# Making the second product of each gate/up pair by seven half-size products

## The reference

```python
def bitlinear(x, w):
    scale = mean(abs(w))
    return x @ (round(clip(w / (scale + EPS), -1, 1)) * scale).T
out = x + bitlinear(bitlinear(y, w_gate) * bitlinear(y, w_up), w_down)
```

## Time and profile before

| | us |
|---|---|
| median of 3 runs (1727.34 to 1729.59) | 1727.45 |
| span of the profiled execution | 1726.1 |
| PE busy | 1707.7 |
| DVE busy | 1096.0 |
| ACT busy | 575.6 |
| POOL busy | 28.0 |

### The profile page before, as it was taken

The page is one execution under the profiler, slowest core; times in us unless marked ns, Lnnn a source line. Parts: engine busy times, 40 slices in busy tenths (PEclk is TensorE's granted clock), DMA queues, the critical chain, the costliest instruction groups (busy, mean ns, idle before and its releaser), DMA issues.

```text
span 1726.1 us, 31355 instructions
## 1 busy us (share of the span) xinstructions
PE 1707.7 (99%) x12424; PEld 1215.6 (70%) x12424; DVE 1096.0 (63%) x1786; ACT 575.6 (33%) x921; POOL 28.0 (2%) x59
## 2 busy tenths in 40 slices
PE   6999999999999999999999999999999999999999
PEld 5554545968769596795958768596776959678684
DVE  6898895555766468554685646755576545855464
ACT  6887732312333133230333213231233313323120
POOL 0010000000000000000000000000000000000000
PEclk9999999999999999999999999999999999999999
DMA  8666626312242032420224211331223313132021
GB/s 342 249 229 239 221 96 219 121 44 97 76 148 96 22 108 77 168 66 22 107 102 164 65 75 54 129 137 43 97 76 126 101 40 108 65 124 79 29 87 49
DMA packets 59735, 194.06 MB, mean 112 GB/s; under 512 B 5280, under 2 KB 5600, under 8 KB 59584
## 3 DMA queue, kind: packets, MB, share of 16 engines
q1 hardware_dynamic: 56432, 177.49, 28.9%
q0 software_dynamic: 2560, 14.36, 2.2%
q10 hardware_dynamic: 592, 0.09, 0.0%
HBM read 160.90 MB, written 31.01 MB: 111 GB/s over the span
## 4 chain that ended last, share of the span: by engine, by line
PE 97%; DVE 2%; DMA 1%; issue 0%; ACT 0%; SPq 0%; DVEq 0%
PE ps L881 52%; PE ps L938 25%; PE ps L658 17%; PE ps L899 2%; PE ps L761 1%; DMA xa<-in_x_dram 1%; DVE wsum L1318 0%; DVE ys L1413 0%; DVE msk L1458 0%; DVE ys L1380 0%; DVE xa L1529 0%; DVE prod L1496 0%; DVE yp L1418 0%; ACT wdT L1106 0%; SPq L493 0%
## 5 line engine op out<-in xcount | busy, mean ns | idle before, releaser
L881 PE MATMUL ps<-yp,wgT 128*128 128x256 f16 x4116 | 902.4, 273 | 1.1 <-issue 1.1
L881 PE MATMUL ps<-wuT,wgT 128*128 128x256 f16 x4116 | 902.4, 273 | 0.0
L881 PEld LDWEIGHTS ps<-yp,wgT 128*128 128x128 fp8e4 x4116 | 402.9, 98 | 50.8 <-issue 2.9
L881 PEld LDWEIGHTS ps<-wuT,wgT 128*128 128x128 fp8e4 x4116 | 402.7, 98 | 48.3
L938 PE MATMUL ps<-wdT,inter 128*128 128x512 fp8e4 x1960 | 433.2, 379 | 0.0
L938 PEld LDWEIGHTS ps<-wdT,inter 128*128 128x128 f16 x1960 | 191.1, 98 | 227.2 <-issue 1.4
L1762 DVE SCALAR_TENSOR_TENSOR xr<-ps,osc,xr 128x512 f32<-128x512 f32 x210 | 156.4, 748 | 168.2 <-PE ps L938 128.4
L1711 DVE TENSOR_TENSOR wdT<-ps,msk 128x512 f32<-128x512 f32 (+1 forms) x77 | 51.3, 666 | 207.1 <-PE ps L881 207.1
L1241 ACT COPY raw<-ps 128x512 f32<-128x512 f32 (+1 forms) x77 | 43.7, 567 | 314.6 <-PE ps L881 314.0
L1248 ACT COPY msk<-ps 128x512 f32<-128x512 f32 (+1 forms) x77 | 43.6, 567 | 138.1 <-PE ps L881 138.1
L1263 ACT COPY inter<-ps 128x256 f32<-128x256 f32 x70 | 26.1, 372 | 180.1 <-PE ps L881 180.1
(11 more groups left out here) (229 smaller groups left out, 1497.9 us busy)
## 6 DMA issues: line engine op xcount, KB each, us to landing
wgT<-wcomb SPq DMA_DIRECT2D x70, 896.0 KB, 4.7
wdT<-dcomb SPq DMA_DIRECT2D x14, 2240.0 KB, 10.9
xa<-in_x_dram SPq DMA_DIRECT2D x8, 2048.0 KB, 7.8
out_dram<-xr SPq DMA_DIRECT2D x64, 256.0 KB, 2.0
wcomb<-xa POOLq DMA_DIRECT2D x17, 448.0 KB, 3.0
xr<-in_L_ffn_w_down_dram SPq DMA_DIRECT2D x9, 512.0 KB, 5.5
inter<-in_L_ffn_w_gate_dram SPq DMA_DIRECT2D x7, 512.0 KB, 16.6
wdT<-in_L_ffn_w_up_dram SPq DMA_DIRECT2D x7, 512.0 KB, 4.4
```

The lines of the kernel that those rows point to most:

```text
L881: last = nc.tensor.matmul(out, w, operand(i, OPERAND[what])[:, k, :], start=(start and h + k + i == 0), stop=(k == KQ - 1 and i == 1), ski ...
```

## The change

From chunk 2 on (`later`), P2 of pairs 0 to 9 is itself split in 2 x 2 blocks: two blocks of 128 outputs, two of depth 256, two halves of 128 tokens. Seven inner products of 2 x 2 matmuls of 128 columns take the place of its 16 matmuls. They are issued in four places of the pair: `inner_a` (two products), `inner_b`, `inner_g` (one each) and `inner_d` (three), into bank ps5 (`IB`) and PA. ScalarE copies a 128-column state of IB after each of the first three, VectorE adds two of them into PA (`inner_upper`). Sums of A12's quarters are made once a chunk by VectorE (`inner_sums`, `inner_lo`) and ScalarE (`hi_inner`). Four sums of weight blocks per pair are made by GpSimd in chunk 1 from the ring and stored in `wsub`; from chunk 2 on SP loads them for each pair (128 KB, `sub_load`) into hi_r or the new buffer sub1, by turns. VectorE's c11 and i11 move behind sum4 of the pair before, the residual copies behind copy_p16, and in pair 0 the first half of P5 goes ahead of P6.

```diff
+    INNER, TH = "P2", P
...
+        upper = wu_flat[:, 4 * KH * TOK + 8 * TOK:4 * KH * TOK + 10 * TOK].bitcast(f32)
+        sub_hl = [b[:, :].bitcast(f16).rearrange("p (s k n) -> p s k n", s=4, k=2) for b in (p2, g_r)]
+        sub_w = [b.rearrange("p (s k n) -> p s k n", s=4, k=2) for b in (hi_r[:, :].bitcast(f8), sub1[:, :])]
...
+        def inner_x(i, s):
+            if s in (IA11, IA12, IA22):
+                k, t = {IA11: (0, 0), IA12: (2, 0), IA22: (2, TH)}[s]
+                return operand(i, OPERAND[INNER])[:, k:k + 2, t:t + TH]
+            return sub_hl[i][:, s - IS1]
+        def inner_w(p, h, kh, k):
+            return ring(p, h, BLOCK[INNER], 2 * kh + k)
...
+            def sub_load(p):
+                dst = (hi_r[:, :].bitcast(f32), sub1[:, :].bitcast(f32))[p % 2]
+                sp.dma_start(dst, wsub[p]).then_inc(s_sub[p % 2], 16)
             def next_pairs(c):
+                if isinstance(c, int) and c == FIRST:
+                    sp.wait_ge(s_subd, NPR)
                 for p, before in ((0, NPR - 1), (1, NPR), (2, NPR - 2)):
...
                     ring_load(p)
+                if isinstance(c, int) and c == FIRST:
+                    for i in range(2):
+                        sp.wait_ge(s_subw[i], 16 * (NPR // 2))
+                sub_load(1)
+                sp.wait_ge(s_ulo, UP * FIRST + 2 * (c - FIRST) + 1)
+                sub_load(0)
...
                     sp.wait_ge(s_m3, NS * (c - FIRST) + p - RING + 1)
+                    if isinstance(c, int) and c == FIRST:
+                        sp.wait_ge(s_subd, p - RING + 1)
                     ring_load(p)
+                    if p - 1 in range(2, NPR) and not (isinstance(c, int) and c == FIRST):
+                        sub_load(p - 1)
                     if p == 8:
...
+            for p in range(NPR):
+                st = sub_stage[p % 2]
...
+                pool.wait_ge(s_ring[p % RING], 16 * (p // RING + 1))
+                if p >= 2:
+                    pool.wait_ge(s_subw[p % 2], 16 * (p // 2))
+                nc.gpsimd.tensor_tensor(st[:, 0], uk[0], gk[0], ALU.subtract, saturate=False).then_inc(s_subt, 1)
...
+                nc.gpsimd.tensor_tensor(st[:, 1], uk[1], st[:, 0], ALU.subtract, saturate=False).then_inc(s_subt, 1)
...
+                nc.gpsimd.tensor_tensor(st[:, 2], uk[1], uk[0], ALU.subtract, saturate=False).then_inc(s_subt, 1)
...
+                nc.gpsimd.tensor_tensor(st[:, 3], gk[1], st[:, 1], ALU.subtract, saturate=False).then_inc(s_subd, 1)
+                pool.wait_ge(s_subd, p + 1)
+                nc.gpsimd.dma_start(wsub[p], p2[:, (p % 2) * HALF:(p % 2 + 1) * HALF]).then_inc(s_subw[p % 2], 16)
             with pool.Fori(2, NC - 1) as c:
...
                     pe.wait_ge(s_c22, n + 1)
-                if p == 0:
+                if p == 0 and half != 1:
                     pe.wait_ge(s_ylo, KH * c + OPERAND[what] + 1)
-                waited(c)
-                for h in range(2 if p < NPR else 1):
+                if half != 1:
+                    waited(c)
+                for h in range(2 if p < NPR else 1) if half is None else (half,):
                     out = bank[:, h * HALF:(h + 1) * HALF]
...
-                last.then_inc(s_done[what], 1)
+                if half != 0:
+                    last.then_inc(s_done[what], 1)
+            def inner(p, out, x, w, start=False):
+                for k in range(2):
+                    for i in range(2):
+                        last = nc.tensor.matmul(out, w[k], inner_x(i, x)[:, k, :], start=(start and k + i == 0),
+                                                stop=(k + i == 2), skip_group_check=True)
+                return last
+            def quarter_w(p, h, kh):
+                return [inner_w(p, h, kh, k) for k in range(2)]
+            def inner_sum_w(p, s):
+                return [sub_w[p % 2][:, s, k, :] for k in range(2)]
+            def inner_a(c, p):
+                n, done = NS * (c - FIRST) + p, DN * FIRST + ND2 * (c - FIRST)
+                pe.wait_ge(s_sub[p % 2], 16 * (NPR // 2 * (c - FIRST - 1) + p // 2 + 1))
+                if p == 0:
+                    pe.wait_ge(s_o, done)
+                    pe.wait_ge(s_ylo, KH * c + OPERAND[INNER] + 1)
+                    pe.wait_ge(s_ilo, c - FIRST)
+                elif p == GRP + 1:
+                    pe.wait_ge(s_o, done + DOWN[0].index(("P2", 1)) + 1)
+                else:
+                    pe.wait_ge(s_c11, n)
+                waited(c)
+                inner(p, IB[:, 0:TH], IA11, quarter_w(p, 0, 0), True)
+                inner(p, IB[:, TH:2 * TH], IS1, inner_sum_w(p, 0)).then_inc(s_ia, 1)
+            def inner_b(c, p):
+                pe.wait_ge(s_e1, NPR * (c - FIRST - 1) + p + 1)
+                waited(c)
+                inner(p, IB[:, 0:TH], IS2, inner_sum_w(p, 1)).then_inc(s_ib, 1)
+            def inner_g(c, p):
+                pe.wait_ge(s_e2, NPR * (c - FIRST - 1) + p + 1)
+                waited(c)
+                inner(p, IB[:, 0:TH], IS3, inner_sum_w(p, 2)).then_inc(s_ig, 1)
+            def inner_d(c, p):
+                pe.wait_ge(s_ir, NPR * (c - FIRST - 1) + p + 1)
+                waited(c)
+                inner(p, PA[:, 0:TH], IA12, quarter_w(p, 0, 1))
+                inner(p, PA[:, 2 * TH:3 * TH], IS4, quarter_w(p, 1, 1))
+                inner(p, PA[:, TH:2 * TH], IA22, inner_sum_w(p, 3)).then_inc(s_m2, 1)
...
+                        elif not (isinstance(c, int) and c == FIRST):
+                            pe.wait_ge(s_ir, NPR * (c - FIRST - 1) + GRP + 1)
...
+                    if p < NPR and not (isinstance(c, int) and c == FIRST):
+                        product(c, p, "P1")
+                        inner_a(c, p)
+                        if p:
+                            product(c, p - 1, "P4")
+                        else:
+                            product(c, p, "P5", 0)
+                        inner_b(c, p)
+                        if more and p - 2 in range(KH):
+                            conv(c + 1, p - 2)
+                        product(c, p, "P6", 0)
+                        inner_g(c, p)
+                        product(c, p, "P6", 1)
+                        product(c, p, "P5", None if p else 1)
+                        if p:
+                            product(c, p - 1, "P3")
+                        inner_d(c, p)
+                        product(c, p, "P7")
+                        continue
...
+                    if s == S4:
+                        hi_inner(c)
...
+            def inner1(c, p):
+                act.wait_ge(s_ia, NPR * (c - FIRST - 1) + p + 1)
+                nc.scalar.copy(PA[:, 0:TH], IB[:, 0:TH]).then_inc(s_e1, 1)
+            def inner2(c, p):
+                act.wait_ge(s_ib, NPR * (c - FIRST - 1) + p + 1)
+                nc.scalar.copy(upper[:, 0:TH], IB[:, 0:TH]).then_inc(s_e2, 1)
+            def inner3(c, p):
+                act.wait_ge(s_ig, NPR * (c - FIRST - 1) + p + 1)
+                nc.scalar.copy(upper[:, TH:2 * TH], IB[:, 0:TH])
+                nc.scalar.copy(PA[:, TH:2 * TH], IB[:, 0:TH]).then_inc(s_e3, 1)
+            def hi_inner(c):
+                act.wait_ge(s_isum, 4 * (c - FIRST))
+                act.wait_ge(s_p2b, c + 1)
+                nc.scalar.copy(sub_hl[0], isums).then_inc(s_ihi, 1)
...
+                    split = p < NPR and not (isinstance(c, int) and c == FIRST)
...
-                    if p < 2:
+                    if split:
+                        inner1(c, p)
+                    if p < 2 and not split:
...
+                    if split:
+                        inner2(c, p)
+                        inner3(c, p)
...
+                    if p < 2 and split:
+                        residual(c, 2 * p)
+                        residual(c, 2 * p + 1)
...
-                    dve.wait_ge(s_i22, NPR * (c - FIRST) + p)
+                    dve.wait_ge(s_i12 if later(c) else s_i22, NPR * (c - FIRST) + p)
...
-                if p:
+                if later(c) and p < NPR:
+                    dve.wait_ge(s_i11, NPR * (c - FIRST) + p + 1)
+                elif p:
...
-                if p < NPR - 1:
+                if later(c) and p < NPR:
+                    dve.wait_ge(s_i22, NPR * (c - FIRST) + p + 1)
+                elif p < NPR - 1:
...
+            def inner_upper(c, p):
+                dve.wait_ge(s_e3, NPR * (c - FIRST - 1) + p + 1)
+                V.tensor_tensor(PA[:, HALF:TOK].rearrange("p (a n) -> p a n", a=2),
+                                upper.rearrange("p (a n) -> p a n", a=2),
+                                IB[:, TH:2 * TH].unsqueeze(1).broadcast_to([P, 2, TH]), ALU.add).then_inc(s_ir, 1)
+            def inner_sums(c):
+                a = quarter(OPERAND[INNER])
+                a11, a12, a21, a22 = (a[:, k:k + 2, t:t + TH] for t in (0, TH) for k in (0, 2))
+                n = 4 * (c - FIRST - 1)
+                dve.wait_ge(s_ysc, KH * c + KH)
+                dve.wait_ge(s_loS, NPR * (c - FIRST))
```

(73 more changed lines are left out.)

## The result

The changed kernel takes **1817.87 us** (median of 4 runs, 1812.58 to 1822.17) against 1728.52 for the kernel before in the same comparison: ratio 1.0517, 95% interval 1.0504 to 1.0529. It is 5.2% slower; 3.3% was forecast, 1785 in a range of 1757 to 1817. The direction and the place were right, the size was not. The profiled execution is the one of 1812.58 us, with a span of 1810.8.

The account below looks back on a forecast made before the run. PE's own queue was taken to bound the kernel. Terms of -11, +36 and +32 made +57 us on the 1726.1 us span, 1783, so a median of 1785 us, 3.3% slower, in a range of 1757 to 1817.

Parts of the forecast that it names:

- 28 small matmuls for 16, 60 times: P2 in chunks 2 to 7: 28 matmuls of 56 ns replace 1.75 us by 1.57, 11.0 us less in all.
- loads 3, 4, 5, 7, 8 behind the ring load, 30 times: SP's queue: weight sums land behind the 896 KB ring load, so inner_a stalls 1.2 us each time, 36 us.
- load 2 behind x, 5 times: Pair 2, chunks 2 to 6: weight sums queue behind x, bias and ring 3; inner_a stalls 6.2 us each.
- load 2 of the last chunk: Pair 2 of the last chunk, which loads no x: a stall of only 1.2 us.
- PE's queue is what counts, and inner_a waits for wsub: PE's work and waits count in full; its one new costly wait is inner_a's for the weight sums, +36 and +32 us.
- The copies and sums hide: New ScalarE copies and VectorE sums in the pairs finish before PE wants them; costed at nothing.
- The small matmuls run at 56 ns: The 128-column inner matmuls start 56 ns apart, their 98-ns weight loads overlapping, as in the trace's transpose bursts.
- rival B: 128-column matmuls paced by 98-ns weight loads: 1837 us, or 1816 by the skill's 81 ns; chance 0.10.
- GpSimd costs nothing: GpSimd's four operations and a transfer per pair, in one chunk only, fit within 13.12 us and add nothing.
- Rival A: The small weight-sum transfer is not held up, lands in 2 us, no stall: 1718 us, faster; chance 0.08.
- C: Sub-load slips in among the ring load's packets: 30 stalls of 0.3 instead of 1.2, load 2 unchanged; 1758 us; chance 0.07.
- granted in full in every slice: TensorE's clock, as read from the profile before the change; no cost for a lower clock entered the sum.

Follow-up runs that it names:

- e5: The e3 kernel with the residual copies of pairs 0 and 1 moved again, so the next x is issued some 9 us earlier; 1720.49 us, ratio 0.9955.
- e1: The changed kernel with sub_load(p-1) issued ahead of ring_load(p) instead of behind it; 1757.31 us, ratio 1.0168.
- e3: The changed kernel with sub_load(p-1) ahead of ring_load(p) for pairs 3 to 9, and load 2 ahead of the next x; 1730.04 us, ratio 1.0012.
- e4: The changed kernel with the weight sums of pairs 2 to 9 issued on ScalarE's queue, ring loads and x left on SP; 1763.89 us, ratio 1.0200.
- e8: The kernel before, with SP made to issue the next x only when P2 of pair 2 is done; 1781.11 us, ratio 1.0309.
- e6: The kernel before, with only the residual copies of pairs 0 and 1 moved behind copy_p16; 1729.82 us, ratio 1.0012.
- e9: The kernel before, with SP made to issue the next x only when P1 of pair 2 is done; 1769.89 us, ratio 1.0246.
- e2: The changed kernel with the residual copies of pairs 0 and 1 back behind copy_p1, so x is issued earlier; 1792.92 us, ratio 1.0365.
- e7: The changed kernel with load 2 alone issued early, ahead of the next x; later loads stay behind their ring loads; 1775.83 us, ratio 1.0274.

## Why the prediction was wrong in size

The ledger of the profiled execution, 1810.8 - 1726.1 = +84.7 us of span. The 36 stalls come to 73.8 + 36 x 0.16 = 79.6.

| term | forecast | measured |
|---|---|---|
| 28 small matmuls for 16, 60 times | -11 | -9.3 (e5) |
| loads 3, 4, 5, 7, 8 behind the ring load, 30 times | +36 | +39.4 |
| load 2 behind x, 5 times | +31 | +39.3 |
| load 2 of the last chunk | +1.2 | +1.0 |
| half clock behind the stalls | not in the sum | +13.9 |
| rest | | +0.4 |

**Right.** *PE's queue is what counts, and inner_a waits for wsub.* 36 waits, in exactly the pairs that were named; none in 0, 1, 6 and 9. e1 and e3 took them away by order alone. *The copies and sums hide.* No wait for inner1 to inner3, inner_upper or c11; in e5 PE is busy for 203.85 of the 203.97 us of chunk 3. *The small matmuls run at 56 ns.* In e5 the 1440 spacings between them have a median of 56 ns (1% to 99%: 55 to 56). The Trainium skill's 81 ns for a sustained stream (page "TensorE: Matmul & The Clock Gate", "Back-to-back issue gap") does not hold here, and rival B is out; runs of 12 are all that was tried. *GpSimd costs nothing:* chunk 1, where it works, lasts 205.1 us before and after. Its operations took 0.65 to 0.81 us; two of the four groups of the changed kernel:

```profile
L703 POOL TENSOR_TENSOR p<-wgT 128x256 fp8e4<-128x256 fp8e4 x10 | 8.1, 812 | 106.3 <-DMA wgT<-wcomb 106.0 <-POOL ablk L273 0.2
L705 POOL TENSOR_TENSOR p<-wgT,p 128x256 fp8e4<-128x256 fp8e4 x10 | 6.4, 645 | 0.8
```

Rival A (the small transfer gets past) and C (it slips in among the ring load's packets) are out in their own queue; e4 shows that something like C happens only from another queue.

**Wrong: the size of load 2's term, "a stall of 6.2 us".** It measured 7.9 us, 1.7 more, 8 us in all. I added the landing of x as the kernel before had it (7.7 us), the bias and ring 3; the time at which PE wants the sums was right to 0.1 us. In the changed kernel x took 8.8 to 9.3 us, ring 3 landed 11.9 to 12.2 us after x was issued where the sum of the parts gave 10.6, and the weight sums 0.3 us behind it, 11.0 us after their own issue. That ring 3 was issued so close behind x does not explain the slow x: in e8 it was as close, 1.1 us, and x took 7.6 to 7.9 us. What goes with a slow x is an instruction fetch of 16 KB (queue q8) in the middle of it. The packets of each queue while x is under way in chunk 2 (number, MB, share of the 16 engines) and the landing of x, in the changed kernel (515.7 to 524.6) and in e8 (534.5 to 542.4):

```profile
q1 hardware_dynamic: 708, 2.50, 80.7%
q8 instruction: 1, 0.02, 0.7%
xa<-in_x_dram SPq DMA_DIRECT2D x1, 2048.0 KB, 8.9
```

```profile
q1 hardware_dynamic: 600, 2.24, 80.3%
xa<-in_x_dram SPq DMA_DIRECT2D x1, 2048.0 KB, 7.9
```

From chunk 1 on, the ten profiles other than e5's hold 60 loads of x. The 32 with such a fetch 4.6 to 6.0 us after issue took 8.7 to 9.4 us, the 28 without one there 7.5 to 8.1. No run moved the fetch by itself, so this is a coincidence in time, not a shown cause. In e8, without it, ring 3 still landed 11.1 to 11.9 us after x was issued: so part of the miss lies in adding the parts, fetch or no fetch. The slow x also goes with the waits for it: 1.7 to 1.9 us in e3, with a fetch each time, against 0.2 to 0.7 us in e6, where x took 7.6 to 8.1.

**Wrong: the step that put no price on the clock.** The prediction read "granted in full in every slice" as if it were a property of the kernel and put no price on an idle PE beyond the idleness. e8 and e9 show the missing term in the kernel before: with a stall of 4.4 to 6.7 us comes a stretch of 3.4 to 10.2 us at 1.2 GHz, part of it over work. In the changed kernel it cost 13.9 us, the largest part of what is missing: its stretches came with all five long stalls and three times again with the 2.3-us stall of pair 3.

**Small: 30 stalls of 1.31 instead of 1.2.** Four of them, in pair 3, were 2.3 us. The trace has a 16 KB instruction fetch of about 1 us on one of the 16 engines just then (it starts at 543.54, where the sum's first share landed at 544.15 and its last at 545.76); in chunk 5 the fetch came 0.5 us later in the transfer, and the stall was 1.1. That the fetch is the cause was not tried here either.

The remaining 5 us of the medians (1817.87, where the profiled run had 1812.58) is the spread between runs of this kernel, 10 us from the first to the last, where the kernel before spreads over 2.4; their granted clocks lie between 0.981 and 0.985. What makes it so wide I leave open.

## What to carry to other kernels

A transfer that is needed soon belongs ahead of those needed late on its queue: the same 128 KB took 1.9 us first and 11.0 last, and a one-line exchange was worth 60 us here. When a change moves a step, count also what its move delays on a queue, as the residual copies delayed x and x the weight sums. Price an idle TensorE above its idleness: from chunk 1 on each of the 22 stalls of 4.4 us and more in these kernels brought 3.4 to 10.2 us at half clock, and so did many of those of 2 to 4.3 us.

## What the runs showed of the hardware

4.4 to 6.7 us without matmuls took the clock from 2.4 to 1.2 GHz, every time (e8, e9), in a kernel that otherwise never left 2.4 from chunk 1 on. Stalls of 3.7 to 4.3 us did so in 4 chunks of 5 (e2, and e4 with 3.9), one of 2.2 us did (e7), and those of 1.7 to 1.9 us alone did not (e3). Matmuls of 128 columns (float16 against fp8 weights, each with its own weight load) started 56 ns apart in runs of 4 to 12, and at 106 ns at half clock. A transfer of 128 KB issued on another queue at the same moment as 896 KB took 4.2 us, against 1.9 alone and 4.5 behind them. 2 MB of x took 7.5 to 8.1 us, and 8.7 to 9.4 where an instruction fetch of 16 KB fell 4.6 to 6.0 us after its issue (60 loads of ten profiles).
